# Split weights stored from another queue, the seam reordered, slot rows of 2304 bytes, a copy ahead of a tanh

## The chip, the cores and the metric

The kernel runs on one core of a Trainium2 chip. The metric is the device time of one execution in microseconds. The engines are TensorE (PE), VectorE (DVE), ScalarE (ACT), GpSimd (POOL) and SyncE (SP); the last only issues DMAs here. Three engines issue DMAs, each on a queue of its own, which the profile writes as SPq, ACTq and POOLq.

## The reference

`x` has 4 batch elements of 1024 tokens and 512 channels, in float32. Four layers follow one another, each added to its input. Expert, subject and category are picked for each batch element by an index that is given with the input.

```python
h = gelu(x @ fc1_w.T + fc1_b)                                  # 512 -> 2048
x = x + concat([h @ fc2_w.T + fc2_b, h @ experts_w[idx].T + experts_b[idx]])   # 384 + 128
x = x + (x @ L1_weight[subject].T + L1_bias[subject])
# the third layer
ctx   = causal_ema(x, tau_ctx)                                 # h = alpha*h + x, along the tokens
wg    = sigmoid(concat([x, ctx]) @ Wg.T + bg);  gated = x * wg
mod   = 0.5 + sigmoid(gelu(x @ Wn1.T + bn1) @ Wn2.T + bn2)      # 4 numbers per token
temporal = sum_d softmax(blend)_d * causal_ema(gated * mod_d, tau_d)            # d = 0..3
gate  = sigmoid(temporal @ Wtemp.T + btemp);  soma = gelu(x @ Wsoma.T + bsoma)
out   = (soma * gate) @ Wout.T
x = x + layernorm(out) * gamma + beta
x = x + (x @ L3_weight[idx] + L3_bias[idx])
```

## The kernel before

The tokens are cut into 8 tiles of 512, two for each batch element; channels lie on the 128 partitions in 4 chunks. Every product is done in three matmuls, with each operand split in a high and a low part: ScalarE writes the high part by a copy, VectorE the low part by a subtraction (`low_part`, L1255), and `split_product` (L979 to L981) multiplies high by high, high by low and low by high. So a 128x512 product of one chunk is three matmuls of 512 columns.

The program has two halves and a seam between them.

The **unit loop** does the first two layers. Unit u = (t, j) takes tile t and block j of 16 hidden blocks: TensorE does `fc1(u)` and, two units behind, `fc2(u-2)`. ScalarE applies the gelu (L844) and copies the high part into h_hl (L848); VectorE subtracts. The products of the L1 layer for tile t-1, its splits and its stores are hung in fixed units of tile t. After x2 (the result of the second layer) is split, GpSimd stores it chunk by chunk to `x2hl_dram` (`store_hl`, L620) and, from an even tile to the next, its last column (L623, a store of 4-byte pieces). SyncE stores x2 itself to `x2_dram` (L455).

In the same loop the weights of the third and fourth layer are prepared: 37 **parked** weights of 128x512. Each is loaded by SyncE into one of two staging tiles (`load_parked`, L416), in some cases changed by VectorE (`parked_made`), split into `stage_hi` and `stage_lo`, and stored in two DMAs (`store_parked`, L630 and L633, on GpSimd's queue, called in the order of the units together with `store_hl`). Staging tiles are used in turn, so the load number n waits until number n-2 has been used up (`staging_free`): for a parked weight until its low part has landed in HBM. One weight kind, WG, needs two loads at once, since VectorE adds the even one and the odd one (L1286). Expert and L1 weights of the next batch element come by the same two tiles.

The second half runs in **rounds** r = 1 to 7. In round r TensorE does n1, the first gate products (`gate`, which write bank(s) that VectorE's scan reads), and the small product `mo` of tile r; then `te` and `ou` of tile r-1 and the last layer `l3` of tile r-2. ScalarE's tanh of mo gives mod_row, which GpSimd changes, stores and loads again as mod_t, spread over the partitions. VectorE does the scans (`scan_g`, `trace_of`), the sums and the low parts: `temporal_low` needs ScalarE's copies `temporal_hi`. `sum_squares` gives sumsq for the layer norm, which TensorE's `ss` waits for.

x2 comes back for these products in six slots, `x2_slot`, each with a high and a low row of LEAD + 512 numbers. The number before the first token lies in LEAD - 1, since the gate reads each row also shifted by one token.

The **seam** is what stands between the two: the last tile's x1, L1 layer and x2, and the traces of tile 0. The order on each engine is the order of the calls in its block; there is no scheduler. `on.wait_ge` puts a wait before the next instruction.

## Time and profile before

| | |
|---|---|
| median of 3 runs | 1424.85 us (1423.33 to 1425.18) |
| the profiled execution | 1430.94 us, its span 1429.0 us |
| mean granted clock of TensorE | 0.988 |
| TensorE busy | 1374.0 us, 96%, 6000 matmuls |
| VectorE busy | 763.0 us, 53% |
| ScalarE busy | 477.7 us, 33% |
| GpSimd busy | 175.8 us, 12% |
| DMA | 140.91 MB, mean 99 GB/s |

A row of the timeline gives the start, the duration, the engine and line, the instruction with the tile that it writes and those that it reads, and in brackets how long the engine had been idle and what ended it. Matmuls are drawn 0.39 us long at the full clock though one starts every 0.227 us, since they are pipelined. Matmuls of float32 count as the program issues them; the granted clock is that of TensorE as the throttle allows it.

### The profile page before, as it was taken

What the parts mean: (1) busy time and instruction counts of PE and PEld (TensorE: products, weight loads), DVE (VectorE), ACT (ScalarE), POOL (GpSimd) and SP (SyncE); (2) the same over time, 40 slices, a digit from 0 to 9 for tenths busy, and PEclk for the clock granted to TensorE, in tenths of its full rate; (3) what the DMA queues carried; (4) which work ended last, traced back from release to release, by engine and by line L of the source; (5) the groups of instructions that cost most, each with busy time, mean ns of one, the idle gap of its engine ahead of it and who ended that gap; (6) DMA issues with size and microseconds to landing.
All of it is one profiled execution on the core that took longest, in us unless ns stands there. A gap on an engine that the chain in (4) does not pass through costs nothing.

```text
span 1429.0 us, 15419 instructions
## 1 busy us (share of the span) xinstructions
PE 1374.0 (96%) x6000; PEld 1119.9 (78%) x6000; DVE 763.0 (53%) x1067; ACT 477.7 (33%) x799; POOL 175.8 (12%) x242
## 2 busy tenths in 40 slices
PE   7999979999989999899999999799999999999998
PEld 6888868888868888688887887578787878787877
DVE  3343323322343332332221666979797979797993
ACT  4443322332232332332321223233334242333353
POOL 5000200100201000200000211012100320032000
PEclk9999989999999999999999999899999999999999
DMA  6522551502732501912323947321232123211201
GB/s 121 140 67 82 147 125 65 166 13 74 154 112 89 155 25 64 212 61 71 91 74 116 207 148 176 119 89 60 89 118 89 59 90 118 89 60 60 89 0 59
DMA packets 63580, 140.91 MB, mean 99 GB/s; under 512 B 7268, under 2 KB 19556, under 8 KB 59540
## 3 DMA queue, kind: packets, MB, share of 16 engines
q1 hardware_dynamic: 50708, 97.30, 23.8%
q0 software_dynamic: 12800, 42.63, 10.2%
q8 instruction: 47, 0.77, 0.2%
q14 instruction: 25, 0.20, 0.1%
HBM read 86.85 MB, written 53.05 MB: 98 GB/s over the span
## 4 chain that ended last, share of the span: by engine, by line
PE 75%; issue 9%; DMA 8%; DVE 5%; ACT 2%; POOL 0%; SPq 0%; DVEq 0%; POOLq 0%; ACTq 0%
PE bank L979 25%; PE bank L981 24%; PE bank L980 24%; DMA stage<-in_fc_w 2%; DMA stage<-in_wg 1%; DVE drive L1411 1%; DMA l3w_dram<-stage_lo 1%; DMA wtemp_dram<-stage_hi 1%; DMA stage<-in_wout 1%; DMA wsoma_dram<-stage_lo 1%; DMA stage<-in_l_w 1%; DVE temporal_lo L1255 1%; DMA wout_dram<-stage_lo 1%; PE bank L1044 1%; DMA wg_dram<-stage_hi 1%
## 5 line engine op out<-in xcount | busy, mean ns | idle before, releaser
L1255 DVE TENSOR_TENSOR h_hl<-bank,h_hl 128x512 fp32r<-128x512 f32 x128 | 88.6, 692 | 439.4 <-ACT h_hl L848 439.4
L979 PE MATMUL bank<-x_hl,wa 128*128 128x512 f32 x512 | 203.4, 397 | 28.5 <-DVE h_hl L1255 21.5
L980 PE MATMUL bank<-x_hl,wa 128*128 128x512 f32 x512 | 202.3, 395 | 0.0
L981 PE MATMUL bank<-x_hl,wa 128*128 128x512 f32 x512 | 201.9, 394 | 0.0
L979 PE MATMUL bank<-h_hl,wa 128*128 128x512 f32 x512 | 199.3, 389 | 0.0
L980 PE MATMUL bank<-h_hl,wa 128*128 128x512 f32 x512 | 199.2, 389 | 0.0
L981 PE MATMUL bank<-h_hl,wa 128*128 128x512 f32 x512 | 199.2, 389 | 0.0
L844 ACT ACTIVATE bank<-bank,small_sb 128x512 f32<-128x512 f32 x128 | 84.1, 657 | 210.4 <-PE bank L981 210.3
L848 ACT ACTIVATE h_hl<-bank 128x512 fp32r<-128x512 f32 x128 | 76.7, 599 | 212.6 <-PE bank L981 211.9
L979 PEld LDWEIGHTS bank<-x_hl,wa 128*128 128x128 f32 x512 | 98.0, 191 | 51.9 <-DVE h_hl L1255 21.6
L981 PEld LDWEIGHTS bank<-x_hl,wa 128*128 128x128 f32 x512 | 98.0, 191 | 20.9
L980 PEld LDWEIGHTS bank<-x_hl,wa 128*128 128x128 f32 x512 | 98.1, 192 | 20.2
L979 PEld LDWEIGHTS bank<-h_hl,wa 128*128 128x128 f32 x512 | 96.1, 188 | 20.3 <-DVE wa L1255 0.3
L981 PEld LDWEIGHTS bank<-h_hl,wa 128*128 128x128 f32 x512 | 96.1, 188 | 20.1
L980 PEld LDWEIGHTS bank<-h_hl,wa 128*128 128x128 f32 x512 | 96.1, 188 | 19.8
L979 PE MATMUL bank<-x_slot,wg_hl 128*128 128x512 f32 x256 | 101.5, 397 | 2.1 <-ACT mod_row L744 2.1
L981 PE MATMUL bank<-x_slot,wg_hl 128*128 128x512 f32 x256 | 100.7, 393 | 0.0
L980 PE MATMUL bank<-x_slot,wg_hl 128*128 128x512 f32 x256 | 100.0, 391 | 0.0
L1396 DVE SCALAR_TENSOR_TENSOR drive<-gated,small_sb,mod_t 128x512 f32<-128x512 f32 x128 | 92.1, 740 | 5.7 <-DMA mod_t<-mod_dram 3.8
L1421 DVE TENSOR_TENSOR temporal<-drive,temporal 128x512 f32<-128x512 f32 x96 | 66.0, 688 | 1.2
L1255 DVE TENSOR_TENSOR x_hl<-x_raw,x_hl 128x512 fp32r<-128x512 f32 x96 | 61.6, 684 | 1.3 <-ACT x_hl L722 1.3
L1411 DVE TENSOR_TENSOR_SCAN drive<-alpha,trace_last,drive 128x512 f32<-128x512 f32 x48 | 60.9, 1268 | 0.0
(162 smaller groups left out, 2315.5 us busy)
## 6 DMA issues: line engine op xcount, KB each, us to landing
x_slot<-x2hl_dram SPq DMA_DIRECT2D x32, 513.0 KB, 4.9
x2hl_dram<-x_hl POOLq DMA_DIRECT2D x28, 512.0 KB, 11.0
stage<-in_l_w SPq DMA_DIRECT2D x32, 256.0 KB, 3.1
x_dram<-x_raw SPq DMA_DIRECT2D x8, 1024.0 KB, 5.6
xt<-x_dram SPq DMA_DIRECT2D x8, 1024.0 KB, 5.7
mod_t<-mod_dram POOLq DMA_DIRECT2D x8, 1024.0 KB, 5.2
l3w_hl<-l3w_dram SPq DMA_DIRECT2D x16, 512.0 KB, 7.9
x_raw<-in_x SPq DMA_DIRECT2D x7, 1024.0 KB, 10.8
```

Of the source, the lines that this page charges most:

```text
L844: eng.activation(ps[:, :], ps[:, :], ACT.Gelu, bias=fc1_b_sb[:, j:j + 1]).then_inc(s_gelu, 1)
L848: eng.activation(h_hl[u % 2][:, 0, :], ps[:, :], ACT.Copy).then_inc(s_hhi, 1)
L979: eng.matmul(ps, w_hi, x_hi, start=first, stop=False)
L980: eng.matmul(ps, w_hi, x_lo, start=False, stop=False)
L981: return eng.matmul(ps, w_lo, x_hi, start=False, stop=final)
L1044: eng.matmul(mo_bank(i)[0:TAUS, :], wn2_sb, h1[:, :], start=True, stop=True).then_inc(s_pe["MO"], 1)
L1255: return eng.tensor_tensor(lo, raw, hi.bitcast(F32), ALU.subtract)
L1396: eng.scalar_tensor_tensor(drive[d % 2][:, :], gated[:, :], blend_sb[:, TAUS * c + d:TAUS * c + d + 1], mod_t[:, d, :], ALU.mult, ALU.mult ...
L1411: eng.tensor_tensor_scan(traced, alpha[:, 1 + d:2 + d].to_broadcast([P, TOK]), drive[d % 2][:, :], start, ALU.mult, ALU.add).then_inc(s_tr ...
L1421: eng.tensor_tensor(temporal[:, c, :], drive[d % 2][:, :], temporal[:, c, :], ALU.add).then_inc(s_add, 1)
```

## The change

Five edits stand in it.

1. `store_parked` moves from GpSimd's program into SyncE's. It is called in `staging_free`, just before the load that reuses the staging tile. The load of x for the next tile goes behind the second weight load of a WG pair.
2. At the start the two index loads go from SyncE to GpSimd, and the four loads of the first x from SyncE to ScalarE's queue.
3. LEAD is 64 in place of 16, so a row of a slot has 2304 bytes in place of 2112. Other tiles are shifted to make room.
4. In each round `temporal_hi(r-1, 3)` stands ahead of `mod_of(r)`.
5. At the seam TensorE does so_pair, two products of l1, n1(1), one of l1, mo(1) and the last of l1, and both first gates after them; n1 and mo of tile 1 write bank 7. VectorE does the scan and traces of tile 0 ahead of x1 and x2 where it can. SyncE loads the slots of tile 1 before xt.

```diff
-        LEAD = 16
+        LEAD = 64
...
         def n1_bank(i):
-            return bank[5 if i else 7]
+            return bank[5 if i > 1 else 7]
...
+            def store_parked(p):
+                n = parked_no(p)
+                on.wait_ge(s_sthi, n + 1)
+                on.wait_ge(s_psthi, 16 * p)
+                eng.dma_start(parked_dram(p)[0], stage_hi[:, :].bitcast(F32)).then_inc(s_psthi, 16)
+                on.wait_ge(s_stlo, n + 1)
+                eng.dma_start(parked_dram(p)[1], stage_lo[n % 2][:, :].bitcast(F32)).then_inc(s_pstlo, 16)
...
             def staging_free(n):
                 if n - 2 in NO_OF_PARKED:
-                    on.wait_ge(s_pstlo, 16 * (NO_OF_PARKED[n - 2] + 1))
+                    p = NO_OF_PARKED[n - 2]
+                    store_parked(p)
+                    on.wait_ge(s_pstlo, 16 * (p + 1))
...
                 load_parked(p + 6)
+                load_parked(p + 7)
                 load_x(2 * b)
-                load_parked(p + 7)
                 load_parked(p + 8)
...
-            load_xt(1)
             for c in range(KC):
                 load_slot(1, c)
+            load_xt(1)
...
                 for j in range(HC):
-                    p = parked_in_unit(t, j)
-                    if p is not None:
-                        store_parked(p)
...
             for r in range(2, NT):
                 h1_of(r)
+                temporal_hi(r - 1, 3)
                 mod_of(r)
-                temporal_hi(r - 1, 3)
...
             so(0, 0)
             so(0, 1)
+            so_pair(0)
             l1(LAST, 0)
             l1(LAST, 1)
-            so_pair(0)
+            n1(1)
             l1(LAST, 2)
+            mo(1)
             l1(LAST, 3)
...
+            scan_g(0, 3)
+            traces_c(0, 2)
             for m in range(KC):
                 x1_of(LAST, m)
             for c in range(KC):
                 x1_lo(LAST, c)
-            traces_c(0, 2)
-            scan_g(0, 3)
             traces_d(0, 2)
-            for m in range(KC):
-                x2_of(LAST, m)
             traces_a(0, 3)
             traces_b(0, 3)
             traces_c(0, 3)
             traces_d(0, 3)
+            x2_of(LAST, 0)
+            x2_of(LAST, 1)
             temporal_low(0)
+            x2_of(LAST, 2)
+            x2_of(LAST, 3)
+            scan_g(1, 0)
             for c in range(KC):
                 x2_lo(LAST, c)
-            scan_g(1, 0)
             traces_a(1, 0)
```

SyncE's queue in the unit loop, tile 1, around the store of x2 (x_dram) and the load of x; stage_57 and stage_58 are the two staging tiles. Before:

```order
L416 DMA stage_57<-in_wsoma 128x512 [waits s_pstlo]
L455 DMA x_dram<-x_raw_52 128x2048 [waits s_x2]
L394 ISA [waits s_pstlo]
L394 DMA stage_58<-in_exp_w 128x512
L416 DMA stage_57<-in_wg 128x512 [waits s_pstlo]
L451 DMA x_raw_52<-in_x 128x2048 [waits s_x2lo,s_x2st]
L416 DMA stage_58<-in_wg 128x512 [waits s_stlo]
```

And after:

```order
L421 DMA stage_57<-in_wsoma 128x512 [waits s_pstlo]
L460 DMA x_dram<-x_raw_52 128x2048 [waits s_x2]
L383 DMA wg_dram<-stage_hi 128x512 [waits s_psthi,s_sthi]
L385 DMA wg_dram<-stage_lo_60 128x512 [waits s_stlo]
L399 ISA [waits s_pstlo]
L399 DMA stage_58<-in_exp_w 128x512
L383 DMA wsoma_dram<-stage_hi 128x512 [waits s_psthi,s_sthi]
L385 DMA wsoma_dram<-stage_lo_59 128x512 [waits s_stlo]
L421 DMA stage_57<-in_wg 128x512 [waits s_pstlo]
L421 DMA stage_58<-in_wg 128x512 [waits s_stlo]
L456 DMA x_raw_52<-in_x 128x2048 [waits s_x2lo,s_x2st]
```

Each pair of stores now stands behind the loads and the store of x2 issued before it, and x stands behind both weight loads.

ScalarE at the start of round 2, where h_70 is the gelu of n1 and mod_row the tanh. Before:

```order
L763 ACTIVATE ts_hi<-temporal 128x512 [waits s_add] x3
L740 ACTIVATE h_70<-bank,small_sb 128x512 [waits s_mst,s_pe_N1]
L744 ACTIVATE mod_row<-bank,small_sb 4x512 [waits s_pe_MO]
L763 ACTIVATE ts_hi<-temporal 128x512 [waits s_add]
L751 ACTIVATE g_last<-bank 128x1 [waits s_g]
```

And after:

```order
L758 ACTIVATE ts_hi<-temporal 128x512 [waits s_add] x3
L735 ACTIVATE h_70<-bank,small_sb 128x512 [waits s_mst,s_pe_N1]
L758 ACTIVATE ts_hi<-temporal 128x512 [waits s_add]
L739 ACTIVATE mod_row<-bank,small_sb 4x512 [waits s_pe_MO]
L746 ACTIVATE g_last<-bank 128x1 [waits s_g]
```

The copy of the fourth chunk no longer stands behind the wait for TensorE's small product.

VectorE at the seam, from the last trace of tile 0 to the spikes; x_raw_53 written from bank and l_b_sb is x2, x_hl_51 its low part. Before:

```order
L1411 SCALAR_TENSOR_TENSOR drive_80<-alpha,drive_80 128x512 [waits s_drive]
L1421 TENSOR_TENSOR temporal<-drive_80,temporal 128x512 [waits s_add,s_trace]
L1255 TENSOR_TENSOR temporal_lo<-temporal,ts_hi 128x1024 [waits s_temphi] x2
L1255 TENSOR_TENSOR x_hl_51<-x_raw_53,x_hl_51 128x512 [waits s_x2hi] x4
L1372 SCALAR_TENSOR_TENSOR bank<-alpha,g_last,bank 128x512 [waits s_glast,s_pe_WG]
L1380 SCALAR_TENSOR_TENSOR gated<-bank,xt_97 128x512 [waits s_xt1,s_wgt]
L1396 SCALAR_TENSOR_TENSOR drive_79<-gated,small_sb,mod_t 128x512 [waits s_tracel,s_mld,s_gated]
```

And after:

```order
L1415 SCALAR_TENSOR_TENSOR drive_80<-alpha,drive_80 128x512 [waits s_drive]
L1425 TENSOR_TENSOR temporal<-drive_80,temporal 128x512 [waits s_add,s_trace]
L1338 SCALAR_TENSOR_TENSOR x_raw_53<-bank,l_b_sb,x_raw_53 128x512 [waits s_pe_L1] x2
L1259 TENSOR_TENSOR temporal_lo<-temporal,ts_hi 128x1024 [waits s_temphi] x2
L1338 SCALAR_TENSOR_TENSOR x_raw_53<-bank,l_b_sb,x_raw_53 128x512 [waits s_pe_L1] x2
L1376 SCALAR_TENSOR_TENSOR bank<-alpha,g_last,bank 128x512 [waits s_glast,s_pe_WG]
L1259 TENSOR_TENSOR x_hl_51<-x_raw_53,x_hl_51 128x512 [waits s_x2hi] x4
L1384 SCALAR_TENSOR_TENSOR gated<-bank,xt_97 128x512 [waits s_xt1,s_wgt]
L1400 SCALAR_TENSOR_TENSOR drive_79<-gated,small_sb,mod_t 128x512 [waits s_tracel,s_mld,s_gated]
```

x2 is now computed behind the traces of tile 0, on both sides of temporal_lo, and the first scan of tile 1 stands ahead of x2's low parts.

## Rows read from the trace of the kernel before

**Rows 1.** The waits of TensorE over the whole span: who waited for whom, us in total, times, longest us.

```profile
PE bank L979 <- DVE h_hl L1255: 21.5, 5, 8.9
PE bank L1147 <- DVE sumsq L1467: 10.6, 1, 10.6
PE bank L979 <- DVE temporal_lo L1255: 8.5, 7, 2.3
PE bank L979 <- DVE x_hl L1255: 7.0, 1, 7.0
```

**Rows 2.** Timeline, TensorE, unit loop: start us, us, instruction, [idle before and its releaser].

```profile
194.04 0.79 PE L979 MATMUL bank<-x_hl,wa 128*128 128x512 f32 x1 [8.92 <-DVE h_hl L1255]
...
198.47 0.55 PE L980 MATMUL bank<-x_hl,wa 128*128 128x512 f32 x1
...
398.74 0.79 PE L979 MATMUL bank<-x_hl,wa 128*128 128x512 f32 x1 [6.37 <-DVE h_hl L1255]
...
602.14 0.79 PE L979 MATMUL bank<-x_hl,wa 128*128 128x512 f32 x1 [5.00 <-DVE h_hl L1255]
```

**Rows 3.** Timeline, VectorE, unit loop.

```profile
159.26 1.28 DVE L1255 TENSOR_TENSOR x_hl<-x_raw,x_hl 128x512 fp32r<-128x512 f32 x2
...
190.72 0.69 DVE L1286 TENSOR_TENSOR stage<-stage,stage 128x512 f32<-128x512 f32 x1 [12.19 <-DMA stage<-in_wg]
...
394.72 0.69 DVE L1291 TENSOR_REDUCE wout_mean<-stage 128x1 f32<-128x512 f32 x1 [9.24 <-DMA stage<-in_wout]
...
599.23 0.29 DVE L1301 TENSOR_TENSOR stage<-stage,ident 128x128 f32<-128x128 f32 x1 [9.26 <-DMA stage<-in_l_w]
```

**Rows 4.** Timeline, SyncE's queue, unit loop.

```profile
177.72 0.33 SPq L416 DMA_DIRECT2D stage<-in_wg  x1
...
178.16 0.37 SPq L451 DMA_DIRECT2D x_raw<-in_x  x1
...
385.20 0.33 SPq L416 DMA_DIRECT2D stage<-in_wout  x1
```

**Rows 5.** Timeline, GpSimd's queue, unit loop.

```profile
163.23 0.71 POOL L620 DMA_DIRECT2D x2hl_dram<-x_hl  x1
...
168.44 0.54 POOL L633 DMA_DIRECT2D wsoma_dram<-stage_lo  x1 [1.06 <-DMA wg_dram<-stage_lo]
```

**Rows 6.** DMA issues of the whole span: KB each, median us from issue to landing.

```profile
stage<-in_wg SPq DMA_DIRECT2D x8, 256.0 KB, 2.9
```

**Rows 7.** Timeline, second round: VectorE, ScalarE and TensorE; last, VectorE and TensorE at sumsq.

```profile
936.53 0.69 DVE L1421 TENSOR_TENSOR temporal<-drive,temporal 128x512 f32<-128x512 f32 x1
...
938.76 0.69 ACT L740 ACTIVATE h<-bank,small_sb 128x512 f32<-128x512 f32 x1 [0.52 <-PE bank L981]
...
947.44 1.23 DVE L1255 TENSOR_TENSOR temporal_lo<-temporal,ts_hi 128x1024 fp32r<-128x1024 f32 x1 [8.40 <-ACT ts_hi L763]
...
948.72 0.51 PE L979 MATMUL bank<-ts_hi,wtemp_hl 128*128 128x512 f32 x1 [1.03 <-DVE temporal_lo L1255]
...
997.09 2.27 DVE L1467 TENSOR_TENSOR sumsq<-bank,sumsq 128x512 f32<-128x512 f32 x3
...
1002.36 0.95 PE L1147 MATMUL bank<-ones,sumsq 128*128 128x1 f32 x8
```

**Rows 8.** Timeline, seam: TensorE, then VectorE.

```profile
861.22 0.50 PE L979 MATMUL bank<-x_slot,wn_hl 128*128 128x512 f32 x1 [0.84 <-DVE x_raw L1334]
...
871.50 0.50 PE L979 MATMUL bank<-x_slot,wg_hl 128*128 128x512 f32 x1 [0.77 <-ACT mod_row L744]
...
883.79 1.41 DVE L1396 SCALAR_TENSOR_TENSOR drive<-gated,small_sb,mod_t 128x512 f32<-128x512 f32 x2 [3.80 <-DMA mod_t<-mod_dram]
...
888.96 0.69 DVE L1453 SCALAR_TENSOR_TENSOR soma<-bank,soma 128x512 f32<-128x512 f32 x1 [1.96 <-ACT bank L768]
```

**Rows 9.** Timeline, TensorE, second round: the first that reads x_slot, and the one behind them.

```profile
958.38 0.40 PE L979 MATMUL bank<-x_slot,wg_hl 128*128 128x512 f32 x1
...
969.45 0.40 PE L979 MATMUL bank<-x_hi,l3w_hl 128*128 128x512 f32 x1
```

More of the change, by code:

```diff
@@ L92, in build @@
                    for s in range(SLOTS)]
-        gated = place("gated", 22.5, [TOK])
-        drive = [place(f"drive{s}", 24.5 + 2 * s, [TOK]) for s in range(2)]
-        sumsq = place("sumsq", 28.5, [TOK])
+        gated = place("gated", 24, [TOK])
+        drive = [place(f"drive{s}", 26 + 2 * s, [TOK]) for s in range(2)]
+        sumsq = place("sumsq", 30, [TOK])
         wg_hl = [place(f"wg_hl{m}", at, [2 * KC, 2, P], F32R) for m, at in enumerate((32, 56, 64, 72))]
@@ L110, in build @@
         wout_hl = place("wout_hl", 184, [KC, 2, DIM], F32R)
-        l3w_at = (152, 156, 200, 120.25)
+        l3w_at = (152, 156, 200, 121)
         l3w_hl = [place(f"l3w_hl{c}", at, [2, DIM], F32R) for c, at in enumerate(l3w_at)]
-        y_sb = [place("y_sb0", 124.25, [TOK]), place("y_sb1", 4, [TOK])]
+        y_sb = [place("y_sb0", 125, [TOK]), place("y_sb1", 4, [TOK])]
         idx = const("idx", 2 * B, I32)
@@ L355, in _ @@
             on = Once(eng)
-            eng.dma_start(idx[0:1, 0:B], tok16).then_inc(s_idx, 16)
-            eng.dma_start(idx[0:1, B:2 * B], tok8).then_inc(s_idx, 16)
             def load_fc1(j):
@@ L365, in _ @@
             load_fc1(0)
-            for c in range(KC):
-                eng.dma_start(x_raw[0][:, c, :], x[0, :, c, :]).then_inc(s_x0[c], 16)
             load_fc1(1)
@@ L592, in _ @@
             on = Once(eng)
+            eng.dma_start(idx[0:1, 0:B], tok16).then_inc(s_idx, 16)
+            eng.dma_start(idx[0:1, B:2 * B], tok8).then_inc(s_idx, 16)
             eng.dma_start(small_sb[:, :], small).then_inc(s_small, 16)
@@ L832, in y_of @@
                                ).then_inc(s_y, 1)
+            for c in range(KC):
+                eng.dma_start(x_raw[0][:, c, :], x[0, :, c, :]).then_inc(s_x0[c], 16)
             fc1_hi(0)
@@ L885, in _ @@
                     x_hi(t + 1, 2 * (j - SPLIT_UNIT) + 1)
+            wg_tanh(0, 3)
             for c in range(KC):
                 x1_hi(LAST, c)
-            soma_of(0, 0)
-            soma_of(0, 1)
-            soma_of(0, 2)
-            soma_of(0, 3)
-            wg_tanh(0, 3)
+            for m in range(KC):
+                soma_of(0, m)
+            for m in range(SH):
+                temporal_hi(0, m)
             h1_of(1)
+            temporal_hi(0, 3)
             mod_of(1)
-            for m in range(KC):
-                temporal_hi(0, m)
             for c in range(KC):
@@ L1033, in n1 @@
                 else:
-                    on.wait_ge(s_x2, KC * NT if i else KC * (LAST - 1) + 2)
+                    on.wait_ge(s_x2, KC * (LAST - 1) + 2)
+                    if i:
+                        on.wait_ge(s_gated, 3)
                 on.wait_ge(s_wn1, 16)
@@ L1057, in gate @@
                 elif m == 1:
-                    if i:
+                    if i > 1:
                         on.wait_ge(s_mod, i + 1)
                     else:
-                        on.wait_ge(s_x2, KC * LAST)
+                        on.wait_ge(s_x2, KC * NT if i else KC * LAST)
                 elif m == 2:
@@ L1071, in gate @@
                         on.wait_ge(s_gated, 3 if i else 2)
+                        if i:
+                            on.wait_ge(s_mod, 2)
                 on.wait_ge(s_wg[m], 16)
@@ L1202, in _ @@
             so(0, 1)
+            so_pair(0)
             l1(LAST, 0)
             l1(LAST, 1)
-            so_pair(0)
+            n1(1)
             l1(LAST, 2)
+            mo(1)
             l1(LAST, 3)
             for r in range(1, NT):
-                n1(r)
+                if r > 1:
+                    n1(r)
                 if r > 1:
@@ L1212, in _ @@
                 gate(r, 0)
-                mo(r)
-                if r == 1:
+                if r > 1:
+                    mo(r)
+                else:
                     gate(r, 1)
@@ L1581, in _ @@
                 x1_lo(LAST, c)
-            traces_c(0, 2)
-            scan_g(0, 3)
             traces_d(0, 2)
-            for m in range(KC):
-                x2_of(LAST, m)
             traces_a(0, 3)
```

10 lines of the change are left out of this document (1 added, 9 removed).

## The prediction

> **What bounds the kernel now.** I read the waits of TensorE first, because the page gives it 96% of the span. Its idle time is in few places: 21.5 us for h_hl, 10.6 us in one wait for sumsq, 8.5 us in seven waits for temporal_lo, 7.0 us at the start [rows 1]. So the time is matmuls at one every 0.227 us plus what TensorE loses in these waits, and an edit pays only where it shortens one of them. VectorE and ScalarE matter where they stand last in a wait.
>
> Next, TensorE's timeline. The wait for h_hl is three gaps of 8.92, 6.37 and 5.00 us, at 194.04, 398.74 and 602.14 [rows 2]. They are one place seen three times, once per batch element whose weights are replaced. After such a gap the granted clock is at its lower level, 1.2 GHz: from 194.04 to 198.47 ten matmuls take 4.43 us in place of 2.27, so 2.2 us more; I take that for all three. Together 20.3 + 6.6 = 26.9 us. VectorE says why: before each gap it waits for a load into stage, 12.19 us for in_wg, 9.24 for in_wout, 9.26 for in_l_w [rows 3]. ScalarE's copy of that weight stands in order ahead of the next gelu, so TensorE runs dry.
>
> Then the queues. SyncE issues a 256 KB weight load at 177.72, a 1 MB load of x at 178.16 and behind it the second weight load [rows 4]; VectorE needs both weights and has them at 190.72. The same kind of load has a median of 2.9 us from issue to landing [rows 6]. In the second gap the load that is waited for was issued at 385.20, ahead of x, and still landed only at 394.72: so x is one half of the cause, and what GpSimd had queued before is the other. There the stores of x_hl go out from 163.23, with parked weight stores in between until 168.44, and that last store had to land before SyncE might issue at 177.72 [rows 4, 5]: 9.3 us.
>
> **The stores on SyncE's queue, and x behind the second load.** 37 parked weights, two stores each, leave GpSimd's queue and go out on SyncE's just before the load that reuses the staging tile. The added instructions are 74 issues of some 0.35 us on SyncE, which has to wait for these very stores anyway; they are hidden while SyncE stands two loads ahead. GpSimd's stores of x_hl have no weight stores in front or between now, and VectorE writes the first two chunks of x_hl from 159.26 [rows 3], so they can start near 160, some 3 us before 163.23, and with no parked pair among them, end 4 to 9 us earlier, an estimate. Against that, on SyncE's queue a parked pair now stands behind the 1 MB store of x2 issued just before. I call these two even for the issue of the awaited load, and leave it at 177.72 and 385.20, the third likewise.
>
> What landing does TensorE need? The end of the load minus the idle time: 190.72 - 8.92 = 181.8; 394.72 - 6.37 = 388.35; 599.23 - 5.00 = 594.2 [rows 2, 3]. The landing after issue is bounded below by the median 2.9 us and above by 9.5 us, which is what the load in front of x took in the second gap. With 2.9 nothing of the gaps is left. With 9.5 the first is 5.4 us, the second stays whole, the third nearly, and with the clock's price only some 3 us are saved. I take 5 us, nearer to the lower row since the backlog on GpSimd's queue ends at least 4 us sooner: gaps of 0.9 and 1.9 us, 1.4 for the third as their mean, 4.2 in all. The gap of 1.03 us at 948.72 brought no lower clock, so no 2.2 is added. Saved: 26.9 - 4.2 = **22.7 us** (3 to 26.9). What is late next is the expert weight one unit before, whose load stands right ahead of these on SyncE's queue; in the kernel before TensorE has no gap there.
>
> The Trainium skill speaks against moving stores at all: "DMA: Bandwidth & Descriptors", section "Issuing engines are not separate DMA queues", has every queue run on the same 16 engines, so that another issuer saves only issue time. By it alone the bytes ahead of the load stay the same and the term would be that of the first rival below.
>
> **The temporal copy ahead of the modulation's tanh.** In each round r from 2 to 7 ScalarE copies the fourth chunk of temporal after the tanh, which waits for TensorE's small product. VectorE's subtraction follows at 947.44 and TensorE stands 1.03 us until 948.72, though the chunk was finished at 936.53 + 0.69 = 937.2 [rows 7]. With the copy ahead, it follows the gelu of 938.76, so temporal_lo is ready near 941, in VectorE's idle 8.40 us [rows 7]. A stall costs its idle time, 0.16 (the last matmul is drawn 0.39 long and the spacing is 0.23) and 0.12 for the slower first step after it: 1.31. Seven waits are counted [rows 1]; the longest, 2.3, is in the tail and stays. Six of 1.31: **7.9 us** (6.2 to 7.9). The tanh moves by one copy of 0.6 us at most where it waits for the product anyway, so at nothing. Next in line is sumsq, which in a round ends at 997.09 + 2.27 = 999.36, 3.0 us before TensorE comes at 1002.36; 1.7 us remain.
>
> **The seam.** After the unit loop TensorE stands 0.84 us before n1 of tile 1 (for x2) and 0.77 before its second gate (for the tanh) [rows 8]. In the new order n1 comes before the last two products of l1 and the small product between them, so gelu and tanh run under l1, and the gates wait for x2 of one product back. Two stalls with their edges, 0.84 + 0.77 + 2 x 0.2 = **2.0 us** (0 to 3.5). All of te moves that much earlier. The 10.6 us before sumsq do not shrink: VectorE reaches its last spikes of tile 0 at 888.96, right behind te, and from there it has the same instructions without a pause. The traces of tile 0 that it does earlier fill idle time ahead of te, since the scan of tile 1 can't start before its gate product. The edit would cost up to 1 us if mod_t were later than te; it came at 883.79 against 888.96 and now starts some 9 us sooner, beside 3 MB of loads and stores, so it has cover.
>
> **The slot rows.** Every read of x_slot by TensorE is a little slower than others: 48 matmuls from 958.38 to 969.45 take 0.2306 us each, the 42 of te from 948.72 to 958.38, less the slow first step, 0.2271 [rows 7, 9]. 96 + 768 + 384 = 1248 such matmuls hold 4.6 us of this. Rows of 2112 bytes become 2304, and the unshifted operand starts as other tiles do. The gain lies between -1 (the reads shifted by one token stay off the boundary) and 4.6; I take **1.5 us**, a third, as nothing shows that the start address is the cause. The Trainium skill, "SBUF — State Buffer", section "Specifications (TRN2)", speaks of lines of 16 bytes only. Both layouts start the unshifted operand on such a line, so by the page this term is 0 and the time 1.5 us higher.
>
> **The start.** x goes out on ScalarE's queue as its first instruction, where it was the fourth DMA on SyncE's, and the two small idx loads go to GpSimd. TensorE begins at 7.0 [rows 1]. ScalarE loads its table only after issuing, and fc1's first weights are issued two DMAs sooner, so x can be split up to 0.9 us earlier, an estimate. But later weight loads fight with GpSimd's 16 tiny stores and don't all move: 0 to 1.0, I take **0.6 us**. The slot loads ahead of xt at the seam cost nothing, as both land before they are read.
>
> **The sum.** 22.7 + 7.9 + 2.0 + 1.5 + 0.6 = 34.7 us. The profiled execution took 1430.94 (span 1429.0 and 1.94 around it), so 1396.2 in a profile like it. The median of the runs is 1424.85, 6.1 lower, by no row that I can name; the same loss there gives **1390.1 us**.
>
> **Rivals.** First: the backlog drains no sooner. The bytes ahead of the awaited load are the same, only the 1 MB of x steps back in the first gap. For it: the load of 385.20 was ahead of x and took 9.5 us. Against it: GpSimd's part starts earlier and holds less. Only 3 us of the 26.9 go, the sum is 3 + 12.0 = 15.0, and the time 1410.
>
> Second: the gain of the rounds is given back. VectorE works through most of a round; if the sumsq wait swallows what te gains, 7.9 falls out: 1398. Against it are the 3.0 us of lead.
>
> Third, slower: SyncE's queue becomes the bottleneck. Each parked pair stands behind the 1 MB store of x2, SyncE waits for it to land before the expert load goes out, and all that follows is late by the same amount, at the three places of the gaps. With d us of delay the gaps grow to 20.3 + 6.6 + 3d, against 12.0 won elsewhere: slower from d = 4.0 on, at d = 5 it is 1424.85 + 15 - 12.0 = 1427.9. For it: the last parked store of 168.44 already took up to 9.3 us. Against: it must lose 4 us although the stores it competed with are gone from its own queue.
>
> The diff not doing what it says shows only for the traces of tile 0: they move but shorten no wait. That is in the sum.
>
> **Chances and range.** Forecast 0.81, backlog 0.11, rounds given back 0.04, slower 0.04. Within the forecast the terms' ends reach from 26.9 + 7.9 + 3.5 + 4.6 + 1.0 = 43.9, which is 1381, to gaps half kept (13) and the rest low, 13 + 7 + 1 - 1 = 20, which is 1405. I give 1379 to 1406. About 0.2%, 3 us, is what a measurement can tell from no change here. Faster 0.94, within 0.02, slower 0.04.
>
> **What would show it.** TensorE's waits for h_hl near 4 us in place of 21.5, each under 2.5, with no slow clock behind them; VectorE's waits for in_wg, in_wout and in_l_w under 6 us. One wait for temporal_lo, that of the tail. The sumsq wait still 10 to 11 us. x_slot matmuls at 0.229 or so. TensorE's first matmul before 6.5. I am wrong if a gap of more than 4 us remains at the load, if ScalarE's new long wait is the expert load one unit before, or if the sumsq wait shrinks.

## Result: 1412.6 us, a ratio of 0.992, outside the range of the forecast

| | median us | lowest and highest | profiled execution | span |
|---|---|---|---|---|
| before | 1424.5 (4 runs) | 1423.3, 1425.2 | 1430.9 | 1429.0 |
| changed | 1412.6 (4 runs) | 1411.7, 1413.4 | 1413.1 | 1411.1 |

The ratio is 0.9917, with a 95% interval of 0.9900 to 0.9934. The forecast was 1390.1 with a range of 1379 to 1406: the sign was right and the gain was a third of what was forecast. The first rival (the backlog drains no sooner, 1410) came nearest in time; the last part shows that this was luck.

First TensorE's waits in the changed kernel (who waited for whom, us in total, times, longest):

```profile
PE bank L1147 <- DVE sumsq L1471: 10.8, 1, 10.8
PE bank L975 <- DVE h_hl L1259: 10.7, 5, 4.3
PE bank L975 <- DVE x_hl L1259: 9.5, 2, 7.9
PE bank L975 <- DVE temporal_lo L1259: 2.5, 1, 2.5
PE bank L975 <- ACT mod_row L739: 1.3, 1, 1.3
PE bank L1158 <- DVE diag L1481: 1.3, 1, 1.3
```

Against [rows 1]: the wait for h_hl is halved and not gone, six of seven waits for temporal_lo are gone, the sumsq wait is what it was, the first matmul is 0.9 us later (7.9), and a wait for diag is new.

TensorE's timeline at the staging gaps (start us, us, instruction, [idle before and releaser]):

```profile
183.86 0.79 PE L975 MATMUL bank<-x_hl,wa 128*128 128x512 f32 x1 [4.30 <-DVE h_hl L1259]
184.46 0.63 PE L976 MATMUL bank<-x_hl,wa 128*128 128x512 f32 x1
...
383.36 0.50 PE L975 MATMUL bank<-x_hl,wa 128*128 128x512 f32 x1 [0.98 <-DVE h_hl L1259]
...
398.04 0.50 PE L975 MATMUL bank<-x_hl,wa 128*128 128x512 f32 x1 [1.55 <-DVE x_hl L1259]
...
586.25 0.80 PE L975 MATMUL bank<-x_hl,wa 128*128 128x512 f32 x1 [4.27 <-DVE h_hl L1259]
```

They answer to [rows 2]. Two gaps of over 4 us remain, one unit earlier than in the kernel before. After the first, steps are 0.43 us apart in place of 0.23: the lower clock again. ScalarE's timeline says what it waits for now, SyncE's queue why:

```profile
170.51 0.63 ACT L675 ACTIVATE stage_hi<-stage 128x512 fp32r<-128x512 f32 x1 [5.53 <-DMA wg_dram<-stage_hi]
...
181.28 0.63 ACT L675 ACTIVATE wa<-stage 128x512 fp32r<-128x512 f32 x1 [8.96 <-DMA stage<-in_exp_w]
```

```profile
158.94 0.43 SPq L460 DMA_DIRECT2D x_dram<-x_raw  x1
...
162.53 0.32 SPq L385 DMA_DIRECT2D wg_dram<-stage_lo  x1
174.19 0.35 SPq L399 DMA_DIRECT2D stage<-in_exp_w  x1
...
182.26 0.81 SPq L421 DMA_DIRECT2D stage<-in_wg  x2
```

The parked pair of 162.53 lands only at 174.0, the expert load behind it goes out then and takes 7 more us. In the kernel before the same load went out at 168.06:

```profile
168.06 0.35 SPq L394 DMA_DIRECT2D stage<-in_exp_w  x1
```

VectorE's wait for in_wg of [rows 3] has shrunk from 12.19 to 2.52 us, those for in_wout and in_l_w from 9.24 and 9.26 to 2.05 and 2.21:

```profile
186.33 0.69 DVE L1290 TENSOR_TENSOR stage<-stage,stage 128x512 f32<-128x512 f32 x1 [2.52 <-DMA stage<-in_wg]
```

This is what the prediction named as its failure: "a gap of more than 4 us remains" and "ScalarE's new long wait is the expert load one unit before".

### The profile page after: what moved, and what is told of

Read it like the earlier page. It is cut to its first block, busy times and chain, and to the rows that moved or that the text cites. A ratio compares the mean times of both kernels' runs of the same rounds, so it can differ in the third digit from the quotient of the medians.

```text
span 1411.1 us, 15375 instructions
## 1 busy us (share of the span) xinstructions
PE 1369.8 (97%) x6000; PEld 1120.5 (79%) x6000; DVE 762.2 (54%) x1067; ACT 478.6 (34%) x799; POOL 136.2 (10%) x170
## 4 chain that ended last, share of the span: by engine, by line
PE 84%; DVE 7%; DMA 6%; ACT 1%; issue 1%; POOL 0%; SPq 0%; DVEq 0%; ACTq 0%; POOLq 0%
PE bank L975 28%; PE bank L976 27%; PE bank L977 27%; DVE drive L1415 2%; DMA wout_dram<-stage_lo 1%; DMA stage<-in_exp_w 1%; DVE drive L1400 1%; DVE temporal L1425 1%; DMA wg_dram<-stage_lo 1%; DMA l3w_dram<-stage_lo 1%; DMA x_slot<-x2hl_dram 1%; DVE temporal L1415 1%; PE bank L1042 1%; PE bank L1147 0%; PE bank L1158 0%
## 5 line engine op out<-in xcount | busy, mean ns | idle before, releaser
L975 PEld LDWEIGHTS bank<-x_hl,wa 128*128 128x128 f32 x512 | 97.5, 190 | 43.6 <-DVE h_hl L1259 11.7
L627 POOL DMA_DIRECT2D x2hl_dram<-x_hl x28 | 21.1, 769 | 627.4 <-DVE x_hl L1259 627.4
```

The costliest lines, as they stand in the source:

```text
L627: eng.dma_start(x2hl_dram[t, c, :, :, 1:1 + TOK], x_hl[t % 2][:, :, c, :].bitcast(F32)).then_inc(s_hlst[c], 16)
L975: eng.matmul(ps, w_hi, x_hi, start=first, stop=False)
```

## Where the time went, stretch by stretch

I cut each execution at the same steps of TensorE: its first step after the second wait of the start (15 to 17 us), the gate product behind the unit loop that waits 1.3 us for mod_row, and the sums of squares of tile 0, of tile 6 (in the last round) and of tile 7 (in the tail). What follows takes 22.6 us in every trace and is left out. All in us:

| profiled kernel | to the start | unit loop | seam | rounds | tail |
|---|---|---|---|---|---|
| before, the forecast's | 15.42 | 762.26 | 148.66 | 442.09 | 37.94 |
| before, second profile | 15.84 | 755.96 | 148.63 | 441.92 | 37.92 |
| changed | 16.10 | 752.29 | 145.97 | 432.28 | 41.92 |
| stores only | 15.74 | 752.04 | 148.67 | 441.49 | 37.94 |
| temporal only | 16.13 | 755.41 | 148.65 | 434.71 | 41.23 |
| slot rows only | 15.98 | 755.24 | 148.06 | 439.41 | 39.54 |
| seam only | 16.23 | 755.78 | 146.72 | 441.60 | 39.53 |
| changed, even rows | 15.96 | 734.50 | 145.99 | 431.54 | 41.06 |
| even rows only | 16.75 | 734.66 | 148.65 | 442.64 | 37.91 |

A loop without staging gaps takes 734.5. So before has 27.8 us of stall (idle and lower clock) in the forecast's profile, 21.5 in the second, and the changed kernel 17.8. Each row is one execution. Kernels with the same code in a stretch agree within 0.2 us in the seam; in the rounds the changed kernel and its variants spread from 431.5 to 434.6, so a difference of 1 or 2 us there is within what one trace can tell.

## Experiments

Theory A was: the gap is at the expert load because its parked pair stands behind the 1 MB store of x2. Rivals: the order of loads matters (B), all 16 engines are busy whatever the order (C), and a part of the stores is slow (E).

**Stores only.** Before, with store_parked moved to SyncE's block; nothing else.

```
 def staging_free(n):            # SyncE
     if n - 2 in NO_OF_PARKED:
-        on.wait_ge(s_pstlo, 16 * (NO_OF_PARKED[n - 2] + 1))
+        store_parked(p)
+        on.wait_ge(s_pstlo, 16 * (p + 1))
 # GpSimd, in unit (t, j)
-        store_parked(p)
```

> The kernel before with one edit: the parked pairs go out on SyncE's queue. Theory A (the pair stands behind the 1 MB store of x2 on that queue, and so the wait moves one unit ahead, to the expert load): TensorE's three long waits become about 4.5 us each and stand one unit earlier, the time is 6 to 9 us below before, 1416 to 1419, and VectorE's long waits for in_wg, in_wout and in_l_w shrink to under 4 us. Theory B (not the queue but the order of p+7 and x is what shortened the gaps in the changed kernel): the gaps stay at 9, 6 and 5 us, the time is within 3 us of before.

Measured: 1420.9, ratio 0.998 (0.9970 to 0.9989). The gaps are 3.8, 3.3 (in three pieces) and 4.7 from one matmul's start to the next, the loop is 752.04. The gaps moved and shrank as A had it, but VectorE's wait for in_wg is 5.3 where A had under 4, and the time is 2 us above A's and just inside B's 3 us: the profile on which A was sized was not typical (below).

**Store of x2 later.**

```
-                store_x2(2 * b - 2)
                 load_exp(b, KC)
+                store_x2(2 * b - 2)
```

> The changed kernel, with the 1 MB store of x2 of tile 2b-2 issued after the expert load in place of ahead of it. Theory A (the parked pair waits behind that store): the pair lands some 5 us sooner, the expert load is out near 169 instead of 174.2, and the gaps of 4.7, 4.0 and 4.7 us fall below 1.5 each; time 1400 to 1404. Theory C (all 16 engines are busy with 3.5 MB whatever the order, so the landing moves little): expert load within 1 us of 174.2, time 1411 to 1414. Theory D (the delayed store delays the load of x behind it): a new wait for x_raw, time over 1414.

Measured: 1412.8, ratio 0.9915 (0.9894 to 0.9936), as the changed kernel. SyncE's queue:

```profile
163.00 0.32 SPq L385 DMA_DIRECT2D wg_dram<-stage_lo  x1
170.69 0.35 SPq L399 DMA_DIRECT2D stage<-in_exp_w  x1
171.08 0.43 SPq L460 DMA_DIRECT2D x_dram<-x_raw  x1
...
183.12 0.81 SPq L421 DMA_DIRECT2D stage<-in_wg  x2
```

The expert load is out 3.5 us sooner and the next loads 0.9 later; the gap of 4.68 becomes three of 2.62, 1.37 and 1.25, and the loop takes 752.34. What one transfer gains another loses: in time the order is worth nothing, and A falls. C holds for the time, though not for the issue of the expert load, which it had within 1 us of 174.2.

**Stores back on GpSimd's queue.** The changed kernel with the stores-only edit reversed, the rest kept.

> The changed kernel with the parked pairs back on GpSimd's queue, all other edits kept. Theory A: the gaps are again those of before, perhaps 2 us smaller at the first, so 6 to 8 us above the changed kernel, 1418.5 to 1420.5. Theory B: the order alone keeps the gaps small, 1411 to 1414.

Measured: 1414.0, ratio 0.9929 (0.9905 to 0.9954). The interval overlaps that of the changed kernel; by the traces the loop is 2.1 us longer (754.37), with gaps of 5.45, 4.51 and 4.10, again at the unit of the kernel before. The time is B's, the place of the gaps is A's. The queue of the parked pairs is worth 2 to 4 us, not 22. x behind the second weight load, which this run keeps, was not run alone; the loop is 0.9 to 1.6 us shorter here than in the kernels without either edit, little more than one trace can tell.

**Even rows.** x2hl_dram is padded so that its rows are 2112 bytes apart; all transfers move the same bytes.

```
-    x2hl_dram = ... [NT, KC, P, 2, 1 + TOK]
+    x2hl_dram = ... [NT, KC, P, 2, 16 + TOK]
```

The stores go to `16:16 + TOK` of a row, the halo to `15:16`, and the loads begin at 15.

> The changed kernel, with rows of x2hl_dram 2112 bytes apart instead of 2052 and the tile's first token at byte 64 of its row, so that the 512 KB stores write to addresses that are multiples of 64; bytes moved are the same. Theory E (in the backlog from 162 to 178 the engines are all busy at only 150 to 240 GB/s because these stores' 2 KB pieces start at odd addresses): the four stores land in 6 to 8 us in place of 11.3, the expert load goes out 3 us sooner, the gaps fall to 1 to 2 us, time 1402 to 1407. Theory F (the addresses do not matter; the rate is that of two queues on the same engines): landing within 1 us of 11.3, time 1411 to 1414.

Measured: **1395.8**, ratio 0.9805 (0.9787 to 0.9822), more than E expected. Three rows of the changed kernel by windows of 5 us (us, busy of PE, PEld, DVE, ACT and POOL, PEclk, DMA share, GB/s), then the same with even rows:

```profile
160.00:165.00 5.00, 5.00 (x24) 4.14 (x23) 2.76 (x5) 2.81 (x5) 2.77 (x4) 1.00 0.96 367
165.00:170.00 5.00, 5.00 (x24) 4.14 (x23) 0.86 (x2) 0.00 (x0) 2.78 (x4) 1.00 1.08 221
170.00:175.00 5.00, 5.00 (x24) 4.14 (x23) 1.38 (x2) 1.78 (x3) 0.00 (x0) 1.00 1.02 164
```

```profile
160.00:165.00 5.00, 5.00 (x23) 4.13 (x22) 2.76 (x5) 2.82 (x5) 2.78 (x4) 1.00 0.97 373
165.00:170.00 5.00, 5.00 (x24) 4.14 (x23) 1.98 (x4) 1.78 (x3) 2.79 (x4) 1.00 0.99 352
170.00:175.00 5.00, 5.00 (x24) 4.14 (x23) 0.15 (x1) 0.41 (x1) 0.00 (x0) 1.00 0.65 201
```

Both are full from 160 to 170. But from 165 on the changed kernel's engines are full (1.08, 1.02) at only 221 and 164 GB/s: they are busy, not with bytes. With even rows they move 352 GB/s from 165 to 170 and are only 65% busy behind that. SyncE's queue with even rows:

```profile
162.41 0.32 SPq L385 DMA_DIRECT2D wg_dram<-stage_lo  x1
168.84 0.35 SPq L399 DMA_DIRECT2D stage<-in_exp_w  x1
...
175.75 0.81 SPq L421 DMA_DIRECT2D stage<-in_wg  x2
```

The second store of the pair lands in 6.3 us in place of 11.5. The page's row of the stores, KB each and median us to landing, in the changed kernel and then with even rows:

```profile
x2hl_dram<-x_hl POOLq DMA_DIRECT2D x28, 512.0 KB, 10.0
```

```profile
x2hl_dram<-x_hl POOLq DMA_DIRECT2D x28, 512.0 KB, 5.3
```

TensorE's wait for h_hl is down to one of 0.8 us:

```profile
PE bank L975 <- DVE h_hl L1259: 0.8, 1, 0.8
```

**Before, profiled again**, without an edit.

> The kernel before, unchanged, profiled a second time. The profiled execution of before on which the forecast rests took 1430.9, 6.4 above the median of 1424.5, while those of the changed kernel lie within 0.5 us of theirs. Theory G (that execution had longer staging gaps than most): here the three gaps, with their edges 9.3, 6.8 and 5.4 us there, together are 5 to 7 us shorter, so about 15, and the execution takes 1423 to 1426. Theory H (the loss is spread over the whole execution, and the gaps are what they were): gaps within 1 us of 21.5 in sum.

Measured: 1424.8, span 1422.8. TensorE at the three gaps:

```profile
191.76 0.80 PE L979 MATMUL bank<-x_hl,wa 128*128 128x512 f32 x1 [7.02 <-DVE h_hl L1255]
...
395.19 0.79 PE L979 MATMUL bank<-x_hl,wa 128*128 128x512 f32 x1 [5.14 <-DVE h_hl L1255]
...
596.51 0.50 PE L979 MATMUL bank<-x_hl,wa 128*128 128x512 f32 x1 [2.41 <-DVE h_hl L1255]
```

Against 8.92, 6.37 and 5.00 in [rows 2] they are 5.7 us shorter, and the loop as a whole 6.3, as G has it: the 6.1 us between the profiled execution and the median lay in the loop, nearly all in these gaps. The other kernels that keep the old stores (temporal only, slot rows only, seam only) have loops of 755.2 to 755.8, as this one.

**Even rows only**: the kernel before with the edit of the even rows.

> The kernel before with one edit: rows of x2hl_dram 2112 bytes apart, data from byte 64; the parked pairs stay on GpSimd's queue. If the rate of these stores alone makes the staging gaps, they vanish as in the run of the changed kernel with even rows (no wait for h_hl over 1 us), and with 15 to 21 us of gaps and 3 to 6 us of slow clock gone the time is 1400 to 1408. If GpSimd's order (parked pairs between the stores) has a part of its own, gaps of 2 to 4 us each stay, and the time is 1409 to 1417.

Measured: 1405.0, ratio 0.987 (0.9853 to 0.9886), loop 734.66. The gaps are gone with the parked pairs still on GpSimd's queue.

**Changed, even rows, stores back on GpSimd's queue**: the edits of "Even rows" and "Stores back" together.

> The changed kernel with even rows (byte 64, 2112 apart), but with the parked pairs back on GpSimd's queue. If the staging gaps were made by the rate of the x2hl stores alone, the queue of the parked pairs no longer matters: within 0.15% of the 1395.8 with them on SyncE's, no wait for h_hl over 1 us. If the pairs between these stores cost something of their own, gaps of 1 to 3 us come back and the time is 1399 to 1404.

Measured: 1395.8, ratio 0.9801 (0.9783 to 0.9820), loop 734.52. With even rows the edit to the queue is worth nothing.

**Changed, even rows, old start.**

```
 # SyncE
+eng.dma_start(idx ...)  x2
 load_fc1(0)
+for c in range(KC): eng.dma_start(x_raw[0][:, c, :], ...)
 # ScalarE and GpSimd: the same lines removed
```

> The changed kernel with even rows and the start of before (x and the idx loads on SyncE's queue). The start costs what the two traces show, first step of the second group of matmuls at 16.10 against 15.42, and the stall of 0.79 at 53.5 that the new start has not: so from 0.1 us slower to 0.9 faster than the changed kernel with even rows (1395.8); if TensorE's first matmul is not back near 7.0, the later start has another cause than the four loads of x being out ahead together with the weight load.

Measured: 1396.4, ratio 0.9813 (0.9796 to 0.9829), not told apart from 1395.8. In the traces TensorE begins at 7.2 in place of 7.8 and its second group at 15.13 in place of 15.96: the new start costs 0.8 us there, and the loop behind it is the same (734.57 against 734.50). In the times the 0.8 us do not show. The four loads of x land after a median of 6.0 us in the changed kernel, 4.4 in the one before.

**Temporal copy only.** Before, with

```
 for r in range(2, NT):          # ScalarE
     h1_of(r)
+    temporal_hi(r - 1, 3)
     mod_of(r)
-    temporal_hi(r - 1, 3)
```

> The kernel before with one edit: in rounds 2 to 7 the copy of temporal's fourth chunk stands ahead of the modulation's tanh. By the forecast six stalls of 1.31 us go: 7.9 us less than before, 1415.5 to 1417.5, and a round's period falls from 73.0 to 71.7. If the gain of a round is given back at sumsq or behind mod_t, the period stays above 72.5 and the time is over 1421.

Measured: 1418.8, ratio 0.9976 (0.9960 to 0.9992), a gain of 3.4 to 4.2 us; only half of the forecast one. The rounds give what they should (442 to 434.7 us, a period of 72.0), but the tail is 3.3 us longer. TensorE there, in the changed kernel (in this one the two waits are the same) and in the second profile of before:

```profile
1354.47 1.13 PE L1158 MATMUL bank<-diag,ones 128*128 128x128 f32 x8 [1.28 <-DVE diag L1481]
1358.11 0.77 PE L975 MATMUL bank<-ts_hi,wtemp_hl 128*128 128x512 f32 x1 [2.51 <-DVE temporal_lo L1259]
1358.67 0.63 PE L976 MATMUL bank<-temporal_lo,wtemp_hl 128*128 128x512 f32 x1
1359.10 0.63 PE L977 MATMUL bank<-ts_hi,wtemp_hl 128*128 128x512 f32 x1
```

```profile
1372.16 0.47 PE L979 MATMUL bank<-ts_hi,wtemp_hl 128*128 128x512 f32 x1 [2.34 <-DVE temporal_lo L1255]
```

VectorE, from its last sums for sumsq to diag, in the second profile of before and then in the changed kernel:

```profile
1357.26 2.27 DVE L1467 TENSOR_TENSOR sumsq<-bank,sumsq 128x512 f32<-128x512 f32 x3
...
1367.76 0.88 DVE L1477 TENSOR_SCALAR diag<-ident,rstd 128x128 f32<-128x128 f32 x4
```

```profile
1343.54 2.27 DVE L1471 TENSOR_TENSOR sumsq<-bank,sumsq 128x512 f32<-128x512 f32 x3
...
1354.04 0.87 DVE L1481 TENSOR_SCALAR diag<-ident,rstd 128x128 f32<-128x128 f32 x4
```

From the end of these sums to diag VectorE takes 8.2 us in both. TensorE takes 6.4 us from its sum of squares (1362.35) to the products on diag (1368.77), since in the tail no n1 lies between. So it needs a lead of VectorE of some 2 us. Before, the lead is 2.8 (1359.53 against 1362.35); in the changed kernel 0.8 (1345.81 against 1346.64), and TensorE waits 1.28 for diag, then 2.51 for temporal_lo (2.34 before). In the changed kernel the te products behind then run at steps of 0.43 us for a while, 13.3 us in place of 11.0; in this one they take 12.6. So of the 4.0 us that the tail of the changed kernel is longer, 2.3 are the lower clock.

**Slot rows only, and seam only.** Before, with one of these (the order of SyncE's slot loads is that of before in both):

```
-LEAD = 16
+LEAD = 64        # and the small tiles moved, as in the change
```

```
 so(0, 0); so(0, 1)              # TensorE; ScalarE and VectorE as in the change
+so_pair(0)
 l1(LAST, 0); l1(LAST, 1)
-so_pair(0)
+n1(1)
 l1(LAST, 2)
+mo(1)
 l1(LAST, 3)
```

> The kernel before with one edit: slot rows of 2304 bytes with the tile's first token at byte 256, and the small tiles moved accordingly. Forecast of this term 1.5 us, what the two traces show by the spacing of x_slot matmuls (230.3 against 228.2 ns over 1248 of them) 2 to 3 us. So 1421 to 1423 where before has 1424, a round's period 0.3 to 0.4 us under 73.2, and a matmul on x_slot 2 to 3 ns nearer to the others of its own trace. If the operand's start has no part, the period stays at 73.1 to 73.2.

> The kernel before with one edit: the seam in the new order. From TensorE's first step after the unit loop (771.80 in the second profile of before) to its sum of squares of tile 0 (920.43) it is 148.63 us there; the forecast takes 2.0 off it, the trace of the changed kernel, 768.39 to 914.36, has 145.97, so 2.66 less. I expect 146.0 to 146.8; if it is over 147.5, the layout or something else in the changed kernel gave part of the gain. The rounds stay at 73.2.

Slot rows: 1422.8, ratio 0.9988 (0.9979 to 0.9998). 2.5 us in the rounds (a period of 72.7 against 73.2) and 0.6 in the seam, 1.6 given back in the tail. Seam: one run of 1424.4; the seam is 1.9 us shorter, where the forecast had 2.0, and the tail 1.6 longer. In both the wait of the tail is the old one (2.3 us idle, none for diag), only the te products behind it run at the lower clock for a while, 12.6 us in place of 11.0. What brings the clock down there in these two and not in the kernel before stays open.

**What of the rows counts.** Seven layouts, all on the changed kernel. Only the declaration of x2hl_dram differs (and for the first four the slice that is loaded). Data is stored from byte 4 of a row in all of them.

```
+ [NT, KC, P, 2, 16 + TOK]      data from byte 4: "even pitch, odd start"
+ [NT, KC, P, 2, 17 + TOK]      rows 2116 apart
+ [NT, KC, P, 2, 8 + TOK]       rows 2080 apart
+ [NT, KC, P, 2, 2 + TOK]       rows 2056 apart
+ [NT, KC, P + 4, 2, 1 + TOK]   rows 2052, chunks further apart
+ [NT, KC, P, 2 * (1 + TOK) + 2]  rows 2052, partitions 4112 apart
+ [NT + 1, KC, P, 2, 1 + TOK]   only what lies behind is displaced
```

> The changed kernel with rows of x2hl_dram 2112 bytes apart, but the data from byte 4 of the row as before, so that every 2 KB piece starts 4 bytes past a multiple of 64. If what slows the stores is a piece that starts and ends off a multiple of 64, nothing is gained against the changed kernel: landing near 10 us median, time 1410 to 1414. If it is only the uneven distance of the rows, it is as with even rows: landing near 5.3, time 1394 to 1398.

> The changed kernel with rows of x2hl_dram 2116 bytes apart, data from byte 4. The starts drift through all offsets of a 64-byte stretch as at 2052, but 68 bytes lie between the end of one row's data and the start of the next, so no two pieces share such a stretch. If sharing is what costs, this is as fast as 2112: landing near 5.3 us, time 1394 to 1398. If the drifting starts cost, it is as slow as the changed kernel: landing near 10, time 1410 to 1414.

> The changed kernel with rows 2080 bytes apart, data from byte 4: the pieces start at 4 or 36 past a multiple of 64, and every second pair of neighbours shares a 64-byte stretch, though no 32-byte one. If shared stretches of 64 bytes cost, about half of the slowdown stays: landing 7 to 8 us, time 1400 to 1406. If only 32 bytes or less count, or only the drift, it is as fast as 2112: 1394 to 1398.

> The changed kernel with rows of x2hl_dram 2056 bytes apart, data from byte 4: 8 bytes between the end of one row's data and the start of the next, so that nearly all neighbours still share a 32-byte stretch (at 2080 and 2116 none did). If the shared stretch is what costs, this is nearly as slow as the changed kernel: landing 9 to 10 us, time 1408 to 1414. If any padding helps, because the rows no longer touch, it is as fast as 2080: 6 us, 1394 to 1398.

> The changed kernel, rows 2052 bytes apart, with 16416 more bytes between the chunks that four stores write at the same time. If the chunks' distance of 525,312 bytes (1024 over a power of two) makes them meet in the memory, this is fast: landing 5 to 7 us, time 1394 to 1399. If it is the rows' own distance, slow as before: landing near 10, 1410 to 1414.

> The changed kernel with the partitions 4112 bytes apart as in the run with rows at 2056, but the two rows of a partition 2052 apart. If the distance from partition to partition counts (each engine writes whole partitions), landing is 6 to 7 us and the time 1394 to 1398. If the gap between two rows counts, half of the gaps are still 4 bytes: landing 8 to 10, time 1400 to 1412.

> The changed kernel with x2hl_dram one tile longer than it is used, all distances inside as in the changed kernel; only the tensors that may lie behind it are displaced, by 2,101,248 bytes. If the place of the tensors counts, it is fast, 1394 to 1399; I expect no effect: landing near 10 us, 1410 to 1414.

| layout | bytes between partitions | landing, median us | unit loop us | time us | before beside it | ratio, 95% |
|---|---|---|---|---|---|---|
| changed | 4104 | 10.0 | 752.3 | 1412.6 | 1424.5 | 0.9900 to 0.9934 |
| chunks apart | 4104 | 10.6 | 757.4 | 1421.0 | 1431.2 | 0.9909 to 0.9959 |
| behind displaced | 4104 | 11.3 | 758.2 | 1419.5 | 1431.2 | 0.9904 to 0.9957 |
| partitions 4112 | 4112 | 7.5 | 737.1 | 1396.2 | 1431.2 | 0.9735 to 0.9781 |
| rows 2056 | 4112 | 6.9 | 735.6 | 1395.8 | 1424.6 | 0.9787 to 0.9826 |
| rows 2080 | 4160 | 6.5 | 734.5 | 1397.1 | 1424.8 | 0.9791 to 0.9826 |
| rows 2112, byte 4 | 4224 | 6.0 | 734.5 | 1396.4 | 1424.3 | 0.9789 to 0.9828 |
| even rows (byte 64) | 4224 | 5.3 | 734.5 | 1395.8 | 1423.8 | 0.9787 to 0.9822 |
| rows 2116 | 4232 | 6.0 | 734.5 | 1396.0 | 1424.8 | 0.9787 to 0.9822 |

For the time, the start of a piece does not matter (byte 4 as good as byte 64, though the stores land after 6.0 us against 5.3), nor that starts drift (2116), nor the chunks' distance, nor where the other tensors lie. My second theory, that neighbouring rows share a stretch of 64 or 32 bytes, fell with 2056: there three quarters of neighbours still share 32 bytes, and it is fast. What is left is the distance from partition to partition: at 4104 bytes all is slow, at 4112 and more it is fast, with the two rows of a partition at 2052 or not. With it goes the room between the data of one partition and the next, 4 bytes at 4104 and 8 or more in the others; since a partition's data is of one size, no run can tell the two apart. Nor is it a plain step: at 4112 a small stall is left in the loop, 1.1 us with rows 2056 and 2.6 with rows 2052 inside, and landing is 6.9 and 7.5 us, one execution each. Chunks apart, behind displaced and partitions 4112 ran on one chip, on which the kernel before takes 1431.2; the fast one takes there what it takes elsewhere, and the slow ones are 7 to 8 us over the changed kernel's 1412.6, with much the same ratio to the kernel before. Why 4104 is slow stays open: no run tells whether it is the memory behind it or the way the 16 engines meet in it.

The Trainium skill, "DMA: Bandwidth & Descriptors", section "How a descriptor splits into AXI transactions", makes pieces that don't start at a multiple of 256 bytes dearer. Here a start at byte 4 costs nothing that shows in the time (1396.4 against 1395.8), and at most 0.7 us of landing. The same page, section "Latency and other measured facts", reports for copies from HBM to HBM a rate halved by a row pitch of 4 MiB, which a padding of 192 bytes does not cure. Here the slow distance is 4 KiB and 8 bytes, and 8 bytes more cure it.

## Why the prediction was wrong, by its own steps

**Staging gaps, 22.7 forecast.** The unit loop of the changed kernel is 10.0 us shorter than in the profile of the forecast, and 3.7 than in the second one. The step that failed is "I call these two even for the issue of the awaited load, and leave it at 177.72 and 385.20", and with it the expert weight one unit before, named as "what is late next" and put at nothing. Most of the rest of this term held in the traces. GpSimd's stores of x_hl start at 160.12, and the last of them, issued at 167.25, lands 13.8 us later at 181.1, where before it was issued at 170.68 and landed 17.0 us later at 187.7 (185.4 in the second profile): 4.3 to 6.6 us sooner, as worked out. The two loads of in_wg land 2.9 and 3.6 us after issue, under the 5 us taken. But they go out at 182.26 and not at 177.72, since SyncE stands before the expert load until its parked pair has landed, 11.5 us after issue, and again before them. The expert load goes out at 174.19 in place of 168.06, 6.1 us later, and TensorE's gap of 4.3 stands at it. That is the mechanism of the third rival (with the store of x2 issued behind it, the load goes out 3.5 us sooner), which had the price too high: after the load came late, what followed it landed sooner.

Under this lies a premise: I took the lateness for a matter of queues, order and bytes ahead. What made a pair of 256 KB stores take 11.5 us is that the 16 engines wrote x2hl_dram slowly, and this the edit leaves as it was; with even rows the same pair takes 6.3 us, the expert load is out at 168.84 and no gap is left. For the 512 KB stores of [rows 5] I had no landing time. The page's two rows, 11.0 us for them against 5.6 for a store of 1 MB, were there to be read:

```profile
x2hl_dram<-x_hl POOLq DMA_DIRECT2D x28, 512.0 KB, 11.0
```

```profile
x_dram<-x_raw SPq DMA_DIRECT2D x8, 1024.0 KB, 5.6
```

The rule of the Trainium skill that I had weighed there ("DMA: Bandwidth & Descriptors", section "Issuing engines are not separate DMA queues"), by which another issuer saves only issue time, was the better guide: the runs put the value of the other queue at 2 to 4 us with the old rows, and at nothing with even ones (1395.8 either way).

The range took the gaps half kept (13) as its low end, though the term's own low end was 3, which it left to the first rival with 0.11. That rival came within 3 us by luck. Its backlog did drain sooner in the trace, and its 3 + 12.0 stands against 3.7 in the loop and 8.0 elsewhere.

**From the profile to the median.** "The same loss there" was wrong: nearly all of the 6.1 us lay in the very gaps that were to go, so they could not be subtracted twice. The second profile has only 21.5 us to give in the loop. This alone made the forecast about 6 us too low. That 1430.94 lies within the 1427 to 1434 that the kernel before takes on the one slower chip may be why; on which chip it was taken is not known.

**Temporal copy, 7.9 forecast.** The mechanism was right: six stalls gone, 7.2 us less in the rounds. The lead of VectorE at sumsq, 2.8 to 3.0 before, is 1.5 to 2.4 in five rounds of the changed kernel, about the 1.7 worked out, but 0.8 in the last. "Next in line is sumsq ... 1.7 us remain" looked at a round only; in the tail the next in line was diag, which needs a lead of some 2 us, and 3.3 us went back there, 1.6 of them by the lower clock. The second rival had the mechanism of giving back, at the wrong place.

**Seam, 2.0 forecast:** 2.66 in the changed kernel, 1.9 alone, the other 0.6 from the slot rows. The sumsq wait is 10.8, unmoved, as said.

**Slot rows, 1.5 forecast:** 3.1 us in seam and rounds, not 0, and half of it kept behind the tail. A matmul on x_slot takes 228.2 ns on the mean in the changed kernel's trace where it took 230.5. That the layout slowed these reads was right and the size too small; whether their start or the length of the row does it is not separated. The upper end of 4.6 us comes out at 4.4 from the forecast's own rows (1248 times 3.5 ns).

**Start, 0.6 gained forecast:** 0.7 us lost against the forecast's profile, 0.3 against the second. x is issued sooner but lands after a median of 6.0 us in place of 4.4, and TensorE begins at 7.9 in place of 7.0. That the loads now share the engines with the first weights is the likely cause, not a shown one.

Summed, against the forecast's own profile: loop -10.0, seam -2.7, rounds -9.8, tail +4.0, start +0.7, which is -17.8 where -34.7 was forecast. Against the second profile: -3.7, -2.7, -9.6, +4.0, +0.3, which is -11.7; the medians have 11.9.

## To carry to other kernels

When transfers are late, look at GB/s beside the share of busy engines before moving them between queues. Here engines full at half the rate came from a layout, and another issuer or another order was worth 4 us at most. Compare the landing time of each kind of store with others of its size; a padding of 8 bytes or more here was worth 17 us on top of the change, more than the five edits together (11.9). Ask of a moved store what now waits for it in order. Before a gap is priced, see whether the profiled execution is as long as the median, and put the difference where the waits vary; and follow a gain through the tail, where the slack of a round is not there.

## What the hardware showed that I had not expected

- Stores of 128 partitions with 4 KB each, beside the kernel's other transfers, land after 10.0 to 11.3 us (median) in the changed kernel and the two variants of it where the partitions are 4104 bytes apart in memory, and after 5.3 to 7.5 at 4112 or more; the whole kernel is 16 to 25 us slower. Padding x2hl_dram alone, with nothing else of the change, beats the change: 1405.0 against 1412.6. With the change it gives 1395.8.
- The same kernel took 1423 to 1425 on four chips and 1431.2 on a fifth. The kernel with partitions 4112 apart took 1396.2 on that one too.
- A short wait can cost nearly as much again behind it, or nothing. In the tail the same idle time of 2.3 us was followed by te products in 11.0 us in four executions (before, twice; stores only; even rows only) and in 12.6 in two (slot rows only, seam only), by granted clock alone. Behind 2.5 us, with the wait for diag ahead, they took 12.3 to 13.8 in all the others.
